# Expert weights of two MoE layers spread over the partitions by DMA loads from DRAM, in place of products with a selecting matrix

## The reference, cut to what matters

```
x = x + xattn0(layernorm(x), ctx)          # 16 heads, context of 154 tokens
x = x + ffn0(layernorm(x))                 # 8 experts, 2 of them per token
x = x + xattn1(layernorm(x), ctx)          # causal self-attention, then cross-attention, then a small MLP
x = x + ffn1(layernorm(x))                 # 32 experts, 6 of them per token, and a shared one

# ffn0: w[t, e] is the softmax over the two best experts of token t, 0 for the others
y[t] = sum_e w[t, e] * (gelu(x[t] @ W1[e] + b1[e]) @ W2[e] + b2[e])
# ffn1: c[t, e] is 2.5 * score / sum of the six scores, 0 for the others
y[t] = shared(x[t]) + sum_e c[t, e] * ((silu(x[t] @ G[e].T) * (x[t] @ U[e].T)) @ Dn[e].T)
```

## Time and profile before

| | us |
|---|---|
| median of three executions | 746.44 |
| lowest, highest | 746.41, 748.8 |
| the profiled execution | 749.23 |
| its span, first to last instruction | 747.1 |
| TensorE busy in the span | 641.2 (86%) |
| VectorE, ACT, POOL busy | 425.5, 344.9, 121.1 |
| mean granted TensorE clock | 0.970 |

### The profile page before, as it was taken

The page is one execution under the profiler, slowest core; times in us unless marked ns, Lnnn a source line. Parts: engine busy times, 40 slices in busy tenths (PEclk is TensorE's granted clock), DMA queues, the critical chain, the costliest instruction groups (busy, mean ns, idle before and its releaser), DMA issues. The chain is left out here.

```text
span 747.1 us, 8219 instructions
## 1 busy us (share of the span) xinstructions
PE 641.2 (86%) x2616; PEld 406.9 (54%) x2616; DVE 425.5 (57%) x1280; ACT 344.9 (46%) x597; POOL 121.1 (16%) x132
## 2 busy tenths in 40 slices
PE   1698888997999798898998888898779988988997
PEld 1454546553665456554555555465456555655664
DVE  4678787673131337352464526647747787557554
ACT  0356565655655366542864348743352413223221
POOL 6112120010112212122112213233000020000000
PEclk9999999999999999899998999999989999999999
DMA  6000002000000000001000000300000000000000
GB/s 225 22 15 7 15 21 100 1 1 1 15 1 1 7 0 1 1 0 64 0 1 0 1 0 1 120 1 0 1 0 1 15 1 0 1 14 1 14 1 14
DMA packets 8058, 12.85 MB, mean 17 GB/s; under 512 B 1105, under 2 KB 6737, under 8 KB 7633
## 3 DMA queue, kind: packets, MB, share of 16 engines
q1 hardware_dynamic: 8016, 12.34, 4.8%
HBM read 11.29 MB, written 1.05 MB: 17 GB/s over the span
## 5 line engine op out<-in xcount | busy, mean ns | idle before, releaser
L1238 PE MATMUL ps<-xThi,w1s 128*128 128x512 f32 x256 | 152.3, 595 | 3.7 <-DVE h L1198 2.5
L1442 PE MATMUL ps<-h,w2s 128*128 128x512 f32 x256 | 130.6, 613 | 0.0
L722 ACT ACTIVATE h<-ps,early 128x512 f32<-128x512 f32 x128 | 87.6, 687 | 90.2 <-PE ps L1240 88.2
L1239 PE MATMUL ps<-xThi,w1s 128*128 128x512 f32 x256 | 103.5, 404 | 0.0
L1240 PE MATMUL ps<-xTlo,w1s 128*128 128x512 f32 x256 | 103.4, 404 | 0.0
L814 ACT ACTIVATE s<-ps 128x512 f32<-128x512 f32 x68 | 40.6, 597 | 127.8 <-PE ps L1240 124.6
L1198 DVE TENSOR_TENSOR h<-s,ps 128x512 f32<-128x512 f32 x68 | 46.6, 685 | 58.4 <-PE ps L1240 42.2
L589 POOL TENSOR_TENSOR acc_o<-acc_o,ty 128x512 f32<-128x512 f32 x32 | 42.3, 1322 | 215.4 <-DVE ty L1032 215.4
L943 DVE TENSOR_REDUCE NM<-ps 128x2 f32<-128x308 f32 x128 | 58.2, 476 | 26.3 <-PE ps L1310 21.1
L1238 PEld LDWEIGHTS ps<-xThi,w1s 128*128 128x128 f32 x256 | 50.3, 196 | 40.7 <-issue 28.4
L1626 PE MATMUL ps<-h,w2s 128*128 128x512 f32 x128 | 66.6, 602 | 0.7 <-DVE h L1203 0.7
(11 more groups left out here) (278 smaller groups left out, 1016.9 us busy)
## 6 DMA issues: line engine op xcount, KB each, us to landing
w2s<-w_dram SPq DMA_DIRECT2D x2, 2048.0 KB, 9.3
raw<-gu_dram SPq DMA_DIRECT2D x4, 512.0 KB, 4.0
x_in<-x_dram SPq DMA_DIRECT2D x4, 256.0 KB, 2.9
w2s<-dn_dram SPq DMA_DIRECT2D x1, 1024.0 KB, 4.8
out_dram<-ty SPq DMA_DIRECT2D x4, 256.0 KB, 2.3
late<-late_dram SPq DMA_DIRECT2D x1, 608.5 KB, 8.6
ctxA<-ctxT_dram SPq DMA_DIRECT2D x4, 128.0 KB, 2.3
ctxC<-ctxT_dram SPq DMA_DIRECT2D x4, 128.0 KB, 2.0
```

Source lines behind the costliest of these rows:

```text
L722: nc.scalar.activation(h32[:, c % HR, :], bank[c % 2], ACT.Gelu, bias=b1T[:, c:c + 1]).then_inc(b_gelu.sem, 1)
L1238: M(dst, w[0], xThi[:, x, :], start=start, stop=False)
L1239: M(dst, w[1], xThi[:, x, :], start=False, stop=False)
L1442: M(bank[2], w2s[:, c * P:(c + 1) * P], h32[:, c % HR, :], start=(c % 4 == 0), stop=(c % 4 == 3)).then_inc(b_y.sem, 1)
```

## The change

The weights are transposed as they are, in float32, and copied to WT (8 rows) and CT (32 rows). SP then stores these rows to a scratch in DRAM (wt_dram, ct_dram), waits for the store, and loads them again, a row into all 128 partitions for an expert of stage B (two buffers WB), and two rows into 64 partitions each for a unit of stage D (four buffers CB). A load waits until its buffer was read: in stage B for L1032 of two experts before, in stage D for L1203 of four units before. The spreading products, their waits, the copies to WB, the selecting matrices and their casts on VectorE (pick0r, pick1r), the doubled weights (WN, CN) and a memset go. L1203 reads CB in SBUF. Planned times of stages B and D (B_CHUNK, D_CHUNK) are shorter, which moves their steps against those of stage C and of the routing. Four semaphores of stage D are now the ones of stage B, counted on (`Signal.then`).

```diff
-B_CHUNK = [1.65, 2.15, 2.15, 2.15]
+B_CHUNK = [1.6, 2.1, 2.1, 2.1]
...
-D_CHUNK = [3.0, 2.9, 2.6, 2.6]
+D_CHUNK = [2.8, 2.6, 2.4, 2.4]
...
-    WN = sb("WN", [P, NT, 2 * E0], F32R)
-    WT = sb("WT", [P, 2, S], F32R)
+    WT = sb("WT", [P, 2, S])
...
-    CN = sb("CN", [P, NT, 2 * E1], F32R)
-    CT = sb("CT", [P, 2, S], F32R)
+    CT = sb("CT", [E1, 2, S])
+    CB = sb("CB", [P, 4, S])
+    CR = CB.shape[1]
+
+    wt_dram = nc.dram_tensor("wt_rows", (2, E0, S), F32, kind="Internal").ap()
+    ct_dram = nc.dram_tensor("ct_rows", (2, E1, S), F32, kind="Internal").ap()
 
...
+        def spread_first(b):
+            yield prepare0_time(b) + PREPARE0[b > 0][7] + 1.2
+            sp.wait_ge(b_wt.sem, b_wt.at(b, 1))
+            if b >= 2:
+                for r in b_wb:
+                    sp.wait_ge(r.sem, r.at(b - 1, 0))
+            sp.dma_start(wt_dram[b % 2], WT[0:E0, b % 2, :]).then_inc(b_rows.sem, 16)
+            for e in range(E0):
+                if e >= 2:
+                    yield chunk_time(b, 4 * (e - 2) + 6.2) + 1.2
+                else:
+                    stored = prepare0_time(b) + PREPARE0[b > 0][7] + 3.3
+                    yield max(stored, chunk_time(b - 1, 4 * (e + E0 - 2) + 6.2) + 1.2) if b else stored
+                if e == 0:
+                    sp.wait_ge(b_rows.sem, b_rows.at(b, 16))
+                if b * E0 + e >= 2:
+                    sp.wait_ge(b_ty.sem, b_ty.at(b, e - 1))
+                sp.dma_start(WB[:, e % 2, :], wt_dram[b % 2, e, :].partition_broadcast(P)).then_inc(b_wb[e % 2].sem, 16)
+
+        def spread_second(b):
+            yield prepare1_time(b) + 21.6
+            sp.wait_ge(d_ct.sem, d_ct.at(b, 1))
+            if b >= 2:
+                for r in d_cb:
+                    sp.wait_ge(r.sem, r.at(b - 1, 0))
+            sp.dma_start(ct_dram[b % 2], CT[:, b % 2, :]).then_inc(d_rows.sem, 16)
+            for n in range(NP1):
+                yield max(prepare1_time(b) + 23.7, unit_time(b, n + 1 - CR) + 3.2)
+                if n == 0:
+                    sp.wait_ge(d_rows.sem, d_rows.at(b, 16))
+                if b * NP1 + n >= CR:
+                    sp.wait_ge(d_h.sem, d_h.at(b, n - CR + 1))
+                pair = ct_dram[b % 2, 2 * n:2 * n + 2, :].unsqueeze(1).to_broadcast([2, I1, S])
+                sp.dma_start(CB[:, n % CR, :], pair).then_inc(d_cb[n % CR].sem, 16)
...
-               *map(load_context1, every), *map(store, every))
+               *map(load_context1, every), *map(store, every), *map(spread_first, every), *map(spread_second, every))
...
-            nc.gpsimd.memset(WT[:].bitcast(F32), 0.0).then_inc(pads.sem, 1)
-            nc.gpsimd.memset(CT[:].bitcast(F32), 0.0).then_inc(pads.sem, 1)
+            nc.gpsimd.memset(WT[:], 0.0).then_inc(pads.sem, 1)
...
-            copy(WT[0:2 * E0, b % 2, :], bank[3 if b else 7][0:2 * E0, :]).then_inc(b_wt.sem, 1)
+            elif b >= 2:
+                act.wait_ge(b_rows.sem, b_rows.at(b - 1, 0))
+            copy(WT[0:E0, b % 2, :], bank[3 if b else 7][0:E0, :]).then_inc(b_wt.sem, 1)
...
-            def spreads():
-                for e in range(E0):
-                    yield chunk_time(b, 4 * e + 1.8 if e else 4.6) + 0.7
-                    act.wait_ge(b_wb_ps.sem, b_wb_ps.at(b, e + 1))
-                    if b * E0 + e >= 2:
-                        act.wait_ge(b_ty.sem, b_ty.at(b, e - 1))
-                    copy(WB[:, e % 2, :], bank[3]).then_inc(b_wb.sem, 1)
...
-            if b == 0:
-                act.wait_ge(pads.sem, NPAD)
-            copy(CT[0:2 * E1, b % 2, :], bank[3][0:2 * E1, :]).then_inc(d_ct.sem, 1)
+            if b >= 2:
+                act.wait_ge(d_rows.sem, d_rows.at(b - 1, 0))
+            copy(CT[:, b % 2, :], bank[3][0:E1, :]).then_inc(d_ct.sem, 1)
...
-            V.tensor_copy(pick0r[:], pick0).then_inc(ones.sem, 1)
...
-            V.tensor_copy(pick1r[:], pick1.unsqueeze(2).to_broadcast([P, E1, I1])).then_inc(late_set.sem, 1)
...
-            dve.wait_ge(b_w.sem, b_w.at(b, 4))
-            V.tensor_copy(WN[:, :, 0:E0], wn[:]).then_inc(b_w.sem, 1)
-            dve.wait_ge(b_w.sem, b_w.at(b, 5))
-            V.tensor_tensor(WN[:, :, E0:2 * E0], wn[:], WN[:, :, 0:E0].bitcast(F32), ALU.subtract).then_inc(b_w.sem, 1)
...
-                dve.wait_ge(b_wb.sem, b_wb.at(b, e + 1))
+                dve.wait_ge(b_wb[e % 2].sem, b_wb[e % 2].at(b, 16 * (e // 2 + 1)))
...
-            step(V.scalar_tensor_tensor(cw[:], tw[:], 2.5, tr[:].unsqueeze(2).to_broadcast([P, NT, E1]), ALU.mult, ALU.mult))
             if b:
                 dve.wait_ge(d_ct_ps.sem, d_ct_ps.at(b, 0))
-            step(V.tensor_copy(CN[:, :, 0:E1], cw[:]))
-            V.tensor_tensor(CN[:, :, E1:2 * E1], cw[:], CN[:, :, 0:E1].bitcast(F32), ALU.subtract).then_inc(d_r.sem, 1)
+            V.scalar_tensor_tensor(cw[:], tw[:], 2.5, tr[:].unsqueeze(2).to_broadcast([P, NT, E1]), ALU.mult, ALU.mult).then_inc(d_r.sem, 1)
...
-                    dve.wait_ge(d_cb_ps.sem, d_cb_ps.at(b, n))
-                    V.tensor_tensor(h, h, bank[3], ALU.mult).then_inc(d_h.sem, 1)
+                    slot, k = (n - 1) % CR, (n - 1) // CR
+                    dve.wait_ge(d_cb[slot].sem, d_cb[slot].at(b, 16 * (k + 1)))
+                    V.tensor_tensor(h, h, CB[:, slot, :], ALU.mult).then_inc(d_h.sem, 1)
...
-            pe.wait_ge(b_w.sem, b_w.at(b, 6))
+            pe.wait_ge(b_w.sem, b_w.at(b, 4))
             claim(k)
             for i in range(NT):
-                last = nc.tensor.transpose(bank[k][0:2 * E0, i * P:(i + 1) * P], WN[:, i, :].bitcast(F32), ident)
+                last = nc.tensor.transpose(bank[k][0:E0, i * P:(i + 1) * P], wn[:, i, :], ident)
...
-                if b == 0:
-                    pe.wait_ge(ones.sem, NONE)
                 claim(3)
-                M(bank[3], b2dup, WT[:, b % 2, :].bitcast(F32), start=True, stop=True).then_inc(b_base_ps.sem, 1)
+                M(bank[3], b2dup, WT[:, b % 2, :], start=True, stop=True).then_inc(b_base_ps.sem, 1)
                 read_by(3, b_base, b_base.at(b, 1))
-                for e in range(E0):
-                    yield chunk_time(b, 4 * e + 1.8 if e else 4.6)
-                    claim(3)
-                    M(bank[3], spread0(e), WT[:, b % 2, :], start=True, stop=True).then_inc(b_wb_ps.sem, 1)
-                    read_by(3, b_wb, b_wb.at(b, e + 1))
...
-                last = nc.tensor.transpose(bank[3][0:2 * E1, i * P:(i + 1) * P], CN[:, i, :].bitcast(F32), ident)
+                last = nc.tensor.transpose(bank[3][0:E1, i * P:(i + 1) * P], cw[:, i, :], ident)
...
-                    if n:
-                        yield unit_time(b, n) + 1.4
-                        if n == 1:
-                            pe.wait_ge(d_ct.sem, d_ct.at(b, 1))
-                            if b == 0:
-                                pe.wait_ge(late_set.sem, NLATE)
-                        claim(3)
-                        M(bank[3], spread1(2 * (n - 1)), CT[:, b % 2, :], start=True, stop=True).then_inc(d_cb_ps.sem, 1)
-                        read_by(3, d_h, d_h.at(b, n))
```

More of the change, by code:

```diff
@@ L95, with __init__, then @@
 class Signal:
-    def __init__(self, sem, per):
-        self.sem, self.per = sem, per
+    def __init__(self, sem, per, first=0):
+        self.sem, self.per, self.first = sem, per, first
     def at(self, b, k):
-        return b * self.per + k
+        return self.first + b * self.per + k
+    def then(self):
+        return Signal(self.sem, self.per, self.at(NB, 0))
 GROUP = 7
@@ L187, in build_program @@
     w_r, w_gate, b1T, b1f = small["wr"], small["wgate"], small["b1T"], small["b1f"]
-    b2dup, pick0, pick1 = full["b2dup"], full["pick0"], full["pick1"]
+    b2dup = full["b2dup"]
     rows = {n: small["row_" + n] for n in ("bq", "bk", "bv", "bo", "b2f", "gamma", "beta")}
     row_br, row_gb = small["row_br"], small["row_gb"]
-    pick0r = sb("pick0r", [P, E0], F32R)
-    pick1r = sb("pick1r", [P, E1, I1], F32R)
     X2 = sb("X2", [P, NB, NT, P])
@@ L396, in build_program @@
         ("b_xT_ps", 1), ("b_xT", 1), ("b_xs", 2), ("b_lg_ps", 1)))
-    b_lg, b_sd, b_ex, b_w = sig("b_lg", 1 + NT), sig("b_sd", 2), sig("b_ex", 1), sig("b_w", 6)
+    b_lg, b_sd, b_ex, b_w = sig("b_lg", 1 + NT), sig("b_sd", 2), sig("b_ex", 1), sig("b_w", 4)
     b_wt_ps, b_wt, b_base_ps, b_base = (sig(n, 1) for n in ("b_wt_ps", "b_wt", "b_base_ps", "b_base"))
-    b_wb_ps, b_wb = sig("b_wb_ps", E0), sig("b_wb", E0)
+    b_rows, b_wb = sig("b_rows", 16), [sig("b_wb0", 16 * E0 // 2), sig("b_wb1", 16 * E0 // 2)]
     b_h_ps, b_gelu, b_y = (sig(n, NC0) for n in ("b_h_ps", "b_gelu", "b_y"))
@@ L418, in build_program @@
     ND = NP1 + 1
-    d_xT_ps, d_xT, d_xs, d_lg_ps, d_sig = (sig(n, k) for n, k in (
-        ("d_xT_ps", 1), ("d_xT", 1), ("d_xs", 2), ("d_lg_ps", 1), ("d_sig", 1)))
-    d_r = sig("d_r", 12 + 4 * NT)
+    d_xT_ps, d_xT, d_xs, d_lg_ps, d_sig = b_xT_ps.then(), b_xT.then(), b_xs.then(), b_lg_ps.then(), sig("d_sig", 1)
+    d_r = sig("d_r", 10 + 4 * NT)
```

(12 more changed lines are left out.)

## The result

The changed kernel takes 839.62 us, the median of four executions from 834.83 to 842.02; the kernel before takes 746.42 us. The ratio is 1.123, with a 95% interval from 1.117 to 1.130: 93 us slower. The profiled execution took 837.49 us, its span is 835.7.

A forecast was written before the change was run, and what follows sets the result against it. TensorE's order was taken as the bound; with loads on two engines, 478.7 us to layer two's loads, 64 loads of 5.9 us (378) and smaller terms summed to 869.7, corrected to 869 us; likeliest case 823 to 939, eight in ten 696 to 935.

The forecast's parts named there:

- The sum: Whole span: 478.7 + 0.4 + 2 + 378 (64 loads of 5.9) + 4 + 6.6 = 869.7; corrections plus 2.1, less 2.8.
- the first row: Rate per DMA engine before: 4.46 MB in 62.9% of 16x20 us, 22.2 GB/s, at 1.9 KB a packet.
- the second row: Upper bound of the rate per DMA engine: 1.50 MB in 92.6% of 64 engine-us, 25.3 GB/s.
- lower bound of 5.2 us: Layer two: shortest time of a load dealt over two engines (5.9, range 5.2 to 7.0), giving 824 us.
- likeliest case: Layer-two loads dealt over two engines, 5.9 us each: 869 us, from 823 to 939; chance 0.70.
- rival (c): Loads also wait on SP behind a store awaiting a pass's end; at most 5 us, counted in the range; no separate chance.
- The term of 19 us: Layer one: products, waits, cast and low clock going sum to 19.4 us, taken as 19 before the second layer.
- the products that also covered a wait take a little back: Layer one: removed products that had covered a wait return a little, taking 19.4 us to 19.
- rival (a): All 16 engines take part, loads hidden: 19+30-4 for new waits in the shifted order, 45 us gained, 701 us; chance 0.20.
- The test I had written for it: Layer one: no wait of L1542 beyond 2.2 us after the transposes of wn.
- Layer two's own 30 us: Layer two: 15.0 us of products plus 15 of 22 us of waits and clock, if weight rows arrive in time.
- POOL's addition: Layer one, pass 0: without the cast L853, POOL's last addition returns to 1.3 us from 2.79, gaining 1.5 us.

The follow-up runs named there:

- the runs without it: The change with D_CHUNK at 5.15 throughout, 849.37 us; also the change with CB of two slots instead of four, 841.25 us.
- that kernel: Against the kernel before: layer one by loads, layer two by products, all step times as before; 728.24 us, ratio 0.976.
- two transfers: The change with each layer-two load cut into two, one per row, outermost count 64; 709.48 us, ratio 0.951 to the kernel before.
- the old lists: B_CHUNK and D_CHUNK of the kernel before put back: 698.34 us with each layer-two load cut into two, 824.35 us in the change itself.
- two loads in flight: The change with two slots in CB instead of four, outermost count still 2; 841.25 us.
- dealt over four engines: The change with each layer-two load spreading four rows over 32 partitions each, outermost count 4; 714.96 us.

## Why the prediction was right, and where it was not

**The mechanism was right.** Two engines move a load of outermost count 2; what they do sets the pace of layer two; the rest follows. Dealt over more engines the same bytes took 709 us (outermost count 64) and 715 (four), where the prediction had 701 and 724; the change as written took 840. By the Trainium skill (DMA: Bandwidth & Descriptors, "Why a DMA increments its semaphore by 16 and not by 1") the number of engines is the largest, at most 16, that divides both outermost counts. The rule had stood untested in the prediction; the shares of 13.5% and 26.2% for counts of 2 and 4 agree with it.

**The size of a load was the main error.** The sum took 5.9 us, 131 KB at 22.2 GB/s, from the first row because its packets were of nearly the right size. Measured: 5.13 us, 131,072 bytes in 5.13 us, 25.6 GB/s. This is the 25.3 of the second row, the one at 92.6% busy. The error is 64 x 0.77 = 49 us. Why the first row reads low isn't shown. Idle engines don't explain it, since it is a rate per busy time; 341 of its 2344 packets are under 512 B. The same division comes out low where the queue never rests, too: 3.10 MB in 13.5% of 16 x 60 us is 23.9 GB/s, where the spacing of the loads says 25.6. That the second row fits may be luck, since its packets are 5.6 KB on the mean.

My lower bound of 5.2 us was thus slightly too high. With 5.13 and all else as forecast the sum gives 820 us, just outside the likeliest case's own range of 823 to 939. The result lay inside it, near its low end, only because the smaller errors below add 15.5 us; that was luck.

**Three smaller errors ran the other way.** The sum stood at 869.7 us of span before its corrections, the trace at 835.7, 34 less:

- The first load of CB was issued at 484.9, not 478.7: 6.2 us more, since layer one had gained less.
- From there to the last multiply the trace has 827.6 - 484.9 = 342.7 us. 64 loads of 5.13 are 328.3, so 14.4 are left where I had 6.4 (0.4, 2 and 4): 8 us more, of which the idle queue at the second and the third turn is some 5 (4.8 by the runs without it); where the other 3 lie was not taken apart. I had written that the stores of weight rows "end long before the first load that is needed". That held while the queue was empty. Behind a queue of loads the store landed 13.7 us after its issue, and SP stood for it. This is rival (c), with its price right, "at most 5 us", but I looked for it at the wrong store, and the sum didn't have it. The first loads, in the timeline of SP:

```profile
484.89 4.58 SPq L543 DMA_DIRECT2D CB<-ct_rows  x3
```

- From the last multiply to the end 8.1 us instead of 6.6, at a clock of 0.77 in the last pass.

6 + 8 + 1.5 - 49 = -33.5.

**Layer one: right in size, wrong for this kernel.** The term of 19 us measures 16.8 (15 to 21) when the order of the work stays as it was. (The trace of that kernel has X's last write 21.9 us earlier than before, but of two executions that lie 4 us over and 2 us under their medians.) In the change X's last write ended at 505.5, against 517.7 before: 12. What failed is the step where I priced the new step times: "the products that also covered a wait take a little back" and, in rival (a), 4 us for "new waits in the shifted order". They cost 11 us with two transfers (698.3 to 709.5) and 15 in the change (824.4 to 839.6). The test I had written for it, no wait over 2.2 us at the transposes of PN, failed with 2.7; with the old lists it is 1.9, and my arithmetic from the earlier trace rows had left 1.8 (3.3 less 1.5). So reading the wait was sound; carrying it over into another order was not.

**Layer two's own 30 us** measure 32 (29 to 35), or 28.5 within layer two by the trace. The waits that the prediction named, of L1575, L1233 and L1612, are gone there, 19.8 us of them. As it said, others took their place: the gate product waited 7.7 us for VectorE's silu x up (0.4 before) and the down product 3.7 us for the multiply by CB (0.7 before). The 0.23 us for a product is exact where nothing else waits: pairs of 2.47 became 2.24.

**POOL's addition** is back at 1.28 us, as forecast, and the 1.5 us for it are right.

**What was to be seen.** The DMA share was 0.13 to 0.14 (0.12 forecast) and rested at the second and third turn, multiplies 5.13 us apart (5.9), a wait for CB in 51 of 64 pairs. The multiply took 0.70 us from SBUF, against 0.69 from PSUM. TensorE was busy 62 to 70% of passes 1 to 3, not about 40%: its clock fell to 0.77 to 0.87, so the same work took longer. As forecast that cost nothing in between, since the loads take longer still. The landing of CB loads, 15 to 25 us, isn't shown in the profile; the stores behind them took 13.7 and 14.3 us. Layer one's passes were 3.6 and 1.5 us shorter and the last 0.4 longer, not 4 to 6 shorter each; with the old lists they are 7.9, 6.2 and 3.9 shorter.

**The other side.** Rival (a) gave 701 us for 16 engines. With the change's lists it is 709.5, with the old ones 698.3. The gain that the change was after is there. One access pattern hides it.

## What to carry to other kernels

Before moving work to DMA, read the outermost count of both patterns of each new transfer: here a count of 2 in place of 64 made 709 us into 840, with the same bytes. Take the pace of a DMA queue from the spacing of equal transfers where there is such a row; bytes over busy share read low here even in a stretch that never rests (23.9 for 25.6 GB/s). When a change edits the numbers by which a planner orders work, run it once with the old numbers: here the new ones cost 11 us, more than half of what one layer gained.

## What the runs showed of the hardware beyond that

- **An issue can take as long as a transfer.** SP's DMA instruction took 0.32 to 0.47 us while the queue was empty. In layer two of the change it took 4.6 us in the median of the loads of CB and 4.9 to 5.0 us in the rows at 723.40 and 728.62 above, about one load's time. With two loads in flight instead of four the same instructions took 0.47 to 0.61 us (loads) and at most 0.43 (stores). With four loads in flight that are dealt over four engines the loads took 0.50 to 0.64 us. This fits a queue that takes only so much for each engine and then holds up SP, with all that is behind it in SP's order; where its limit lies was not measured.
- **A short transfer is late behind long ones, even if it is dealt otherwise.** The store of the output, 256 KB from 128 partitions, landed 14.3 us after its issue in the change (median), 6.7 with two loads in flight, 4.1 with loads over four engines, and 2.3 us in the kernel with two transfers. The two lines of the change, for this store and that of the weight rows:

```profile
out_dram<-ty SPq DMA_DIRECT2D x4, 256.0 KB, 14.3
...
ct_rows<-CT SPq DMA_DIRECT2D x4, 64.0 KB, 13.7
```

- **Two engines ran at 25.6 GB/s each and four at 65.5 KB in 2.56 us, the same 25.6.** Whether a row of 2 KB is read 64 times or 32 times over made no difference.
- **The clock followed the waits, or the other way round.** Within layer one's passes 1 to 3 TensorE's waits at the transposes of PN and at the product w2s came to 22.1 us with two transfers and the change's lists, and to 9.7 with the old lists; the clock was 0.96 to 0.98 and 0.98 to 1.00. The change itself has 22.3 us of these waits and a clock of 0.95 to 0.96, so they are not all there is to it. Cause and effect were not told apart.
